# Width-one attention: queries and keys in one product over 128 partitions, and a shorter overflow test in the FP8 rounding

## What is computed

```
qkv = jnp.einsum('bnc,fc->bnf', x, w_qkv)
q, k, v = jnp.split(qkv, 3, axis=-1)          # each [b, n, 64]; a head is one column
dots = jnp.einsum('bhid,bhjd->bhij', q, k) * scale
dots = jnp.where(causal, dots, -jnp.inf)
attn = jax.nn.softmax(dots, axis=-1)
out = jnp.einsum('bhij,bhjd->bhid', attn, v)
return jnp.einsum('bnh,ch->bnc', out, w_out)
```

## Time and profile before

| what | us |
|---|---|
| median of 3 runs | 3184.69 |
| fastest and slowest of them | 3184.56, 3190.02 |
| the profiled execution | 3187.42 |
| its span (first to last instruction) | 3185.5 |
| mean granted TensorE clock, share of 2.4 GHz | 0.964 |
| L2_attn, groups of batches 0 to 7 in the trace, about | 1753 to 2045 |

### The profile page before, as it was taken

How to read it: one execution, slowest core, us unless ns; L and a number is a source line. 1 busy time by engine, 2 the same in 40 slices (tenths; PEclk the granted TensorE clock), 3 DMA queues, 4 the chain that set the end, 5 groups by cost and what they waited for, 6 DMA issues and landing times.

```text
span 3185.5 us, 52273 instructions
## 1 busy us (share of the span) xinstructions
PE 2957.7 (93%) x20671; PEld 1962.3 (62%) x20671; DVE 1873.6 (59%) x6456; ACT 1253.8 (39%) x1944; POOL 431.2 (14%) x458
## 2 busy tenths in 40 slices
PE   7999999988989889988998899998999999998998
PEld 4666666865555456655665556566667666766653
DVE  5534343699999447775678768574243444434455
ACT  2222222336555433323443668644233333323443
POOL 0010010124343310000000346410000000000000
PEclk9999999999999999999999779899999999998999
DMA  3000000010000100000000010100000000000000
GB/s 128 1 1 0 1 0 1 1 52 2 1 1 2 34 32 1 1 5 1 1 2 10 19 35 21 48 2 27 1 1 1 1 0 1 1 0 9 2 1 27
DMA packets 22028, 37.75 MB, mean 12 GB/s; under 512 B 2132, under 2 KB 19733, under 8 KB 20760
## 3 DMA queue, kind: packets, MB, share of 16 engines
q1 hardware_dynamic: 20968, 34.02, 3.2%
q10 hardware_dynamic: 816, 0.39, 0.1%
HBM read 26.81 MB, written 2.10 MB: 9 GB/s over the span
## 4 chain that ended last, share of the span: by engine, by line
PE 77%; DVE 16%; ACT 4%; issue 2%; DMA 0%; SPq 0%; DVEq 0%; POOL 0%; ACTq 0%; POOLq 0%
PE ps L414 45%; DVE arena L567 4%; PE ps L619 2%; PE ps L3040 2%; PE ps L2356 2%; PE ps L515 2%; PE ps L3059 2%; PE ps L2310 2%; PE ps L685 2%; ACT arena L673 2%; PE ps L1590 2%; PE ps L726 2%; DVE arena L1924 2%; PE ps L2913 1%; PE ps L552 1%
## 5 line engine op out<-in xcount | busy, mean ns | idle before, releaser
L414 PE MATMUL ps<-weights,arena 128*128 128x256 f32 (+4 forms) x2480 | 694.9, 430 | 41.5 <-DVE arena L1805 26.1
L414 PEld LDWEIGHTS ps<-weights,arena 128*128 128x128 f32 (+1 forms) x2480 | 462.8, 196 | 205.4 <-issue 94.2
L414 PE MATMUL ps<-arena,weights 128*128 128x256 f32 (+4 forms) x1726 | 562.3, 474 | 14.8 <-DMA weights<-in_w_L_attn 6.1
L414 PEld LDWEIGHTS ps<-arena,weights 128*128 128x128 f32 (+1 forms) x1726 | 317.4, 192 | 219.1 <-issue 155.8
L414 PE MATMUL ps<-arena 128*128 128x256 f32 (+4 forms) x1618 | 426.6, 417 | 6.0 <-ACT arena L4758 1.5
L414 PEld LDWEIGHTS ps<-arena 128*128 128x128 f32 (+2 forms) x1618 | 298.1, 188 | 115.1 <-issue 74.7
L567 DVE TENSOR_REDUCE arena<-ps 128x16 f32<-128x1232 f32 (+2 forms) x96 | 179.1, 1865 | 145.3 <-PE ps L545 47.9
L673 ACT ACTIVATE arena<-ps 77x2048 f32<-77x2048 f32 (+1 forms) x112 | 210.0, 1875 | 120.4 <-PE ps L619 58.4
L1924 DVE MATCH_REPLACE8 arena<-arena 128x77 f32<-128x77 f32 x1024 | 214.4, 225 | 0.0
L2323 ACT ACTIVATE arena<-ps 128x1536 f32<-128x1536 f32 x128 | 185.6, 1451 | 70.4 <-PE ps L2312 63.9
L854 POOL TENSOR_TENSOR x<-x,weights 128x512 f32<-128x512 f32 x32 | 43.8, 1370 | 1201.1 <-DVE arena L820 1153.3
(11 more groups left out here) (429 smaller groups left out, 4452.1 us busy)
## 6 DMA issues: line engine op xcount, KB each, us to landing
arena<-arena SPq DMA_DIRECT2D x156, 32.0 KB
weights<-in_w_L_ffn SPq DMA_DIRECT2D x1, 3848.0 KB, 11.6
weights<-in_w_L_attn SPq DMA_DIRECT2D x1, 3840.0 KB, 15.0
weights<-in_w_L_xattn SPq DMA_DIRECT2D x3, 1024.0 KB, 6.3
weights<-in_w_L_ffn SPq DMA_DIRECT2D x1, 3072.0 KB, 9.9
x<-in_x SPq DMA_DIRECT2D x2, 1024.0 KB
weights<-in_w_L_xattn SPq DMA_DIRECT2D x1, 2048.0 KB, 7.4
out<-x SPq DMA_DIRECT2D x8, 256.0 KB, 2.2
```

Source lines behind the costliest of these rows:

```text
L414: ins = k.nc.tensor.matmul(out, lhsT, rhs, start=start and i == 0, stop=i == n - 1)
```

## The change

1. Queries and keys become one product: 128 columns of `wqkv` as weights, queries on partitions 0 to 63, keys on 64 to 127, 256 columns. The copy is 128 x 256 instead of 64 x 512, the scans read partitions 64 to 127 and write 0 to 63.
2. The bounds are folded: tokens 0 to 127 on partitions 0 to 63, tokens 128 to 255 on partitions 64 to 127, by two instructions of 64 x 128. The block to split is 128 x 384 instead of 64 x 768.
3. The bounds' rows take two DMAs for each part instead of one (24 for a batch, 15 of them in ACT's list for batch 0), with pieces of 256 B instead of 512 B.
4. In batches 2 to 5 the bound parts stand at groups 9, 13, 13, 14, 15 instead of 9, 10, 13, 13, 14.
5. `kmax` and `kmin` get places of their own; a gap keeps every later buffer where it was.
6. The rounding's last part is two instructions instead of four: multiply by 2^128/464 (which overflows just where rounding does) and by 0, and add. `f_step` and `f_prep` count two fewer.

```
+OVERFLOW = 2.0 ** 128 / 464
 def round_last_vector(k, link, power, near, out):
     v = k.nc.vector
-    link(v.tensor_tensor(power, near, near, ALU.mult))
-    link(v.tensor_scalar(power, power, 448.0 ** 2, BIG, ALU.is_gt, ALU.mult))
-    link(v.tensor_scalar(power, power, BIG, 0.0, ALU.mult, ALU.mult))
+    link(v.tensor_scalar(power, near, OVERFLOW, 0.0, ALU.mult, ALU.mult))
     return v.tensor_tensor(out, power, near, ALU.add)
...
-ROWS_DMAS = 2 * PAIRS + PARTS
+ROWS_DMAS = 2 * PAIRS + 2 * PARTS
...
-            parts=c.take(PARTS, 3, SEQ, dt=BF16), qkm=c.take(3, SEQ), rest=c.take(3, SEQ)
+            parts=c.take(PARTS, SEQ + P, dt=BF16), qkm=c.take(SEQ + P), rest=c.take(SEQ + P),
+            kmax=c.take(SEQ), kmin=c.take(SEQ), gap=c.take(832)
...
 def rows_of_part(k, s, eng, n, i, queues):
+    q, key = s.parts[0:NH1, i, 0:SEQ], s.parts[NH1:P, i, 0:SEQ]
     for j in range(PARTS):
         if "k" in queues:
-            eng.dma_start(krows[PARTS * i + j:P:PAD, :, :], part[:, 1, :]).then_inc(rows, 16)
+            eng.dma_start(krows[PARTS * i + j:P:PAD, :, :], key).then_inc(rows, 16)
         if "q" in queues:
-            eng.dma_start(qrows[PARTS * j + i:P:PAD, :, :], part[:, 0, :]).then_inc(rows, 16)
+            eng.dma_start(qrows[PARTS * j + i:P:PAD, :, :], q).then_inc(rows, 16)
     if "q" in queues:
-        eng.dma_start(qrows[PAIRS + i:P:PAD, :, :], part[:, 2, :]).then_inc(rows, 16)
+        for half in (0, 1):
+            eng.dma_start(qrows[PAIRS + i:P:PAD, :, half * P:(half + 1) * P],
+                          s.parts[half * NH1:(half + 1) * NH1, i, SEQ:SEQ + P]).then_inc(rows, 16)
...
 def step_qk_tensor(k, pe, s, n, b):
     pe.wait_ge(*s.sig.at("zT", 0, n, 1))
-    for i in (0, 1):
-        ins = proj_feature(k, k.ps[0:NH1, b, i * SEQ:(i + 1) * SEQ], w_of(k, s.stage, "wqkv", KC), s.zT[n % 2],
-                           i * NH1, NH1)
-    ins.then_inc(*s.sig.up("qk_ps"))
+    proj_feature(k, k.ps[:, b, 0:SEQ], w_of(k, s.stage, "wqkv", KC), s.zT[n % 2], 0, 2 * NH1).then_inc(*s.sig.up("qk_ps"))
...
-    v.tensor_copy(s.qkm[0:NH1, 0:2, :], cut(k.ps[0:NH1, b, :], c=2)).then_inc(*s.sig.up("qk"))
+    v.tensor_copy(s.qkm[:, 0:SEQ], k.ps[:, b, 0:SEQ]).then_inc(*s.sig.up("qk"))
...
-        v.tensor_tensor(out, kmax, kmin, ALU.min).then_inc(*done)
+        for half in (0, 1):
+            at = slice(half * P, (half + 1) * P)
+            ins = v.tensor_tensor(s.qkm[half * NH1:(half + 1) * NH1, SEQ:SEQ + P], kmax[:, at], kmin[:, at], ALU.min)
+        ins.then_inc(*done)
...
-    x, rest, parts = s.qkm[0:NH1], s.rest[0:NH1], s.parts[0:NH1]
+    x, rest, parts = s.qkm, s.rest, s.parts
...
-BOUND_AT = (9, 10, 13, 13, 14)
+BOUND_AT = (9, 13, 13, 14, 15)
```

More of the change, by code:

```diff
@@ L1036, in fp8_signals @@
 def fp8_signals():
-    return dict(f_norm=13, f_z=1, f_zT_ps=1, f_zT=1, f_step=9, f_q=1, f_out_ps=1, f_scaled=1, f_shifted=1)
+    return dict(f_norm=13, f_z=1, f_zT_ps=1, f_zT=1, f_step=7, f_q=1, f_out_ps=1, f_scaled=1, f_shifted=1)
 def fp8_buffers(c):
@@ L1134, in turned_two_plan @@
                     done=1, stats=1, **narrow_signals(a), **narrow_signals(b), **fp8_signals())
-    s.ready = Signals(k.signals, st, 1, 1, f_prep=27, f_kernel=1)
+    s.ready = Signals(k.signals, st, 1, 1, f_prep=25, f_kernel=1)
     k.stats_ready["L1_ffn"] = s.sig.at("stats", 0, B - 1, 1)
@@ L2241, in width_one_plan @@
     two = (0, 1)
-    s = Bag(stage=st, z=c.take(2, D), zT=[c.take(KC, SEQ) for _ in two], parts=c.take(PARTS, 3, SEQ, dt=BF16),
-            qkm=c.take(3, SEQ), rest=c.take(3, SEQ), v=[c.take(2, NH1) for _ in two], seen=c.take(P),
+    s = Bag(stage=st, z=c.take(2, D), zT=[c.take(KC, SEQ) for _ in two], parts=c.take(PARTS, SEQ + P, dt=BF16),
+            qkm=c.take(SEQ + P), rest=c.take(SEQ + P), kmax=c.take(SEQ), kmin=c.take(SEQ), gap=c.take(832),
+            v=[c.take(2, NH1) for _ in two], seen=c.take(P),
             krows=[c.take(16, SEQ, dt=BF16) for _ in two],
@@ L2249, in width_one_plan @@
     assert low.at <= HALF, low.at
-    s.kmax, s.kmin = s.rest[:, 0, :], s.rest[:, 1, :]
     s.sig = Signals(k.signals, st, B, 1, z=1, zT_ps=1, zT=1, qk_ps=1, qk=1, v_ps=1, v=1, put=2, parts=PARTS, s_ps=GROUPS,
@@ L2272, in rows_of_part @@
     rows = s.moved.sems["rows"][0]
-    part, qrows, krows = s.parts[0:NH1, i], s.qrows[n % 2], s.krows[n % 2]
+    qrows, krows = s.qrows[n % 2], s.krows[n % 2]
+    q, key = s.parts[0:NH1, i, 0:SEQ], s.parts[NH1:P, i, 0:SEQ]
     eng.wait_ge(*s.sig.at("parts", 0, n, i + 1))
@@ L2486, in step_qk_scalar @@
     act.wait_ge(*s.sig.at("qk_ps", 0, n, 1))
-    k.nc.scalar.activation(s.qkm[0:NH1, 0:2, :], cut(k.ps[0:NH1, b, :], c=2), ACT.Copy).then_inc(*s.sig.up("qk"))
+    k.nc.scalar.activation(s.qkm[:, 0:SEQ], k.ps[:, b, 0:SEQ], ACT.Copy).then_inc(*s.sig.up("qk"))
 def step_v_scalar(k, act, s, n, b):
@@ L2541, in step_qk_vector @@
         dve.wait_ge(*s.sig.at("parts", 0, n - 1, PARTS))
-    v.tensor_copy(s.qkm[0:NH1, 0:2, :], cut(k.ps[0:NH1, b, :], c=2)).then_inc(*s.sig.up("qk"))
+    v.tensor_copy(s.qkm[:, 0:SEQ], k.ps[:, b, 0:SEQ]).then_inc(*s.sig.up("qk"))
 def step_bound_vector(k, dve, s, n, i):
     v, done = k.nc.vector, s.sig.up("split")
-    q, key, out = (s.qkm[0:NH1, j, :] for j in range(3))
+    q, key = s.qkm[0:NH1, 0:SEQ], s.qkm[NH1:P, 0:SEQ]
     kmax, kmin = s.kmax[0:NH1], s.kmin[0:NH1]
```

## The result

| what | us |
|---|---|
| kernel before, median of 6 runs (lowest, highest) | 3185.57 (3184.44, 3190.02) |
| changed kernel, median of 6 runs (lowest, highest) | 3206.55 (3204.84, 3214.23) |
| ratio, 95% interval | 1.0069 (1.0056 to 1.0081) |
| the profiled execution of the changed kernel, its span | 3209.55, 3207.7 |

The change makes the kernel 21 us, or 0.7%, slower. The forecast was 3162 and the range ended at 3189: wrong in sign, and outside.

A forecast was written before the change was run, and what follows sets the result against it. PE was taken to bound, DVE only in short stretches before the clock falls. Terms 0.25 - 0.6 - 1.84 - 1.4 - 16.7 - 0.94 - 2.8 + 1.2 = -22.8 took 3187.42 to 3164.6, median 2.7 below: 3162 us, range 3154 to 3189.

The forecast's parts named there:

- halved product of queries and keys: TensorE step of each batch, eight records become four: saves 0.94 us at full clock, 1.54 for batch 4 at low clock.
- rival C: Slower, clock doesn't come back behind the shortened products: one miss 3183 us, chance 0.08; two or more, 3208, chance 0.10.
- term of -16.7: Batch 1's means to batch 4's product: no clock fall, so 37.8 us at low level become 21.1 at full.
- C's +6.3: First miss, batch 1 group 8: the 11.4 us from 1827.4 to 1838.8, with 2.9 of waits, run low.
- Product at full clock: Products of batches 5, 6 and 7, with PE full: each saves 0.94 us, 2.8 together.
- Batch 3's product and DVE up to the means: Batch 3's halved step saves 1.84 us; shorter copy and rounding save 1.4 of PE's 2.34 us wait at the means.
- ACT's extra DMAs: Start of L2_attn, batch 0: three more row DMAs push ACT's first exponentials by 1.75 us; first wait ends 0.25 later.
- DVE around 1803: Copy, bounds and rounding before PE's waits of 1.75 and 0.39 us: together -0.6 us, bounds 0 and -1.3.
- Copy and bounds: DVE: copy of queries and keys falls from 0.68 to 0.41 us; the bounds' last part, now two instructions, adds 0.1.
- Split: DVE, five instructions from 768 to 384 columns: -2.2 us of DVE for a batch, 0 on the path.
- From batch 1's to batch 2's product: Start of L2_attn: ACT's DMA push takes the 1.8 us PE and DVE save; first wait ends 0.25 us later.
- sum with the clock as before: Rival A, the clock falls as before: terms sum to -7.9 us, 3177 us (3173 to 3180), chance 0.30.

The follow-up runs named there:

- E1: Changed kernel with the product of queries and keys done twice in every batch: 3188.5 us, ratio 1.0007.
- E2: Changed kernel with the product of queries and keys done twice for batch 4 alone: 3183.49 us, ratio 0.9996.
- E3: Kernel before with the shorter rounding alone, the product keeping its two halves: 3173.96 us, ratio 0.9963.
- E6: Kernel before with the shorter rounding and the second scan of batch 1's bounds at group 13: 3165.89, 3168.06 and 3170.92 us, ratio 0.9939.
- E4: Changed kernel with the old rounding, so the attention part alone: 3209.4 us, ratio 1.0057.
- E5: Changed kernel with the second scan of batch 1's bounds moved from group 11 to 13: 3210.89 us, ratio 1.0074.
- E8: E6 with batch 6's rounding cut into smaller pieces spread over three groups: 3177.46 us, ratio 0.9972.

## Why the prediction was wrong

**What failed.** Two steps of the working, both about the clock. The larger: the halved product of queries and keys was counted by its own length alone (-0.94 or -1.54), as if the clock came back behind it as it had behind the whole one. Behind batch 4's it did not, and the row up to batch 5's product came out at +21.9 instead of -0.94. The working had this as rival C and gave it too small a chance.

The other is the term of -16.7 for a fall that would not come ("with 1.4 us less of waiting this one is no longer such a stretch, so I expect no fall"). Where -15.5 was foreseen, -0.6 came. The wait did shrink, 2.34 to 1.19 us, and PE was busy 2.11 of 3.30 us instead of 1.47; the clock fell behind it. One pair of examples had been read as if it set a boundary. E1 and E2 have the same wait (1.19) with a fall, E3 shows one of 1.17 without; E6 has one of 0.67 without and E3 one of 0.68 with one. None of these numbers predicts a fall. Had this term held, there would have been no low stretch for batch 4's step to end, and neither loss.

**The rival that came true.** C had the mechanism and nearly the price: a second miss was costed at "17.3 x 16/11 = 25 more", and it was 21.9 + 1.54 (what the step was to save there at the low level), 23.4; E2 says 23.1 by the medians, and 21.0 by its row from batch 4's to batch 5's product. It had the place a batch early: its first miss was to be batch 3's and its second batch 4's; in the profiled execution batch 3's step brought the clock back and batch 4's did not. In E4 and E5 both missed, as C had it, and there the first miss can be priced: from batch 3's to batch 4's product 51.5 us in both, 46.1 in the changed kernel, so 5.4. C's +6.3 does not follow from the numbers beside it (8.5 us of work at 17.3 in 20.5 give 7.2). Its total of 3208 is 1.5 us from the median, partly by luck: it has a miss of batch 3 (6.3 us) that the trace does not show, and does not have the 5.5 us that this execution already had at batch 1's product.

**What misled on its chance.** C got 0.10 for two misses. The argument against it was that the clock rose 1.5 us into a step of 2.73, so 1.84 us should do. A time inside a step at which the clock rises is no proof that the step up to there was the reason. The counter-evidence was cited too: nothing rose behind the 1.97 us step of values, and the halved step came out at 2.08. By the table above it brings the clock back about one time in two, so that, seen afterwards, with two low stretches that end on such a step a miss was the likelier outcome. The rule of the Trainium skill ("TensorE: Matmul & The Clock Gate", Part 1), that the throttled state is the default and activity releases it, pointed to the right side. The traces go together with its first half as far as the low stretches begin behind waits of PE (here 1.19 us). With its second they do not, as it stands: PE was busy 51.00 of 51.00 us from 1880, and nothing was released.

**The terms that held.**
- *Product at full clock*, -0.94: 30.30 to 29.49 between batches 6 and 7, -0.8. That four matmuls with 128 columns cost what four with 64 did holds: behind the first of a step each takes 377 to 380 ns at full clock and 634 at the low one, as before; the first takes 483 (430 before) and 796 (689). So the steps are 2.08 where 1.84 was foreseen and 1.13 where 0.94 was.
- *Batch 3's product and DVE up to the means*, -3.24: measured -3.2. Within it the wait ended at 1.19, not 0.9, and PE came to it sooner.
- *ACT's extra DMAs*: first exponentials 15.19 us behind batch 1's product instead of 13.61, +1.6 for 1.75 foreseen; taken up as worked out: PE, early by the shorter step, waited 3.78 us for the row DMAs (1.48 before). Up to the L727 at 1767.68 it is 19.77 us, 19.64 before: +0.1 for +0.25. The pieces of 256 B had no price that these traces show: from the end of ACT's last row DMA issue to the first scores it is 1.73 us, 2.75 before.
- *DVE around 1803*, -0.6: -0.5. The forms differ: one wait of 2.93 in place of 1.75 and 0.39.
- *Copy and bounds*: 0.42 for 0.41. Two minima take 0.83 us together on average (6.6 in eight batches) in place of 0.67, +0.16 for +0.1; in batch 2 it is 0.59 in place of 0.73.

**Sized wrong, off the path.** *Split*: the first cast takes 627 ns in place of 821, all five instructions together 3.5 us in place of 4.8: -1.3 for a batch, not -2.2.

**A small miss.** From batch 1's to batch 2's product +0.25 was foreseen and +1.0 came. Beside the start's +0.1, the step of tokens out at 1781.08 took 3.60 us instead of the 2.73 at 1775.41, since here the clock came back 3.3 us into the step, at 1784.4. It is again a term of the clock that the sum did not have.

**What the halves are worth.** Rounding alone: -11.3 us (E3). Attention alone: +24.1 by the median, about 0 at its lower level (E4). Both: +21.0. Both, with one step lengthened again: -1.8 (E2). The sum with the clock as before, 3177, is 6.5 below E2. Of this, 1.5 is batch 4's step, which E2 has in its old length; what makes up the other 5 is open. Nor do the halves simply add up: each changes what the other finds of the clock, and single executions of one kernel spread over 12 us and more (E1, E2, E3).

**Left open.** Why the same step, of the same length, brings the clock back in some executions and not in others; why the wait of 0.67 or 0.68 us is followed by a fall in one kernel and not in the other; what the other executions of the changed kernel lost, of which only one was profiled; and the 5.3 us by which that one was already late before the first changed instruction, in stages where the code is the same.

## What to carry to other kernels

Before a dense TensorE step (matmuls over all 128 rows, back to back) is made shorter, look at the granted clock around it: if the clock comes back behind that step, the step is worth what lies after it at low clock (here 22 us), not its own length (1.6). Cost both outcomes, and treat a single place where the clock held or rose as one example and no boundary. A part that looks small and lies on another engine (two DVE instructions, 1.11 us together) can be worth ten times its length if it shortens a low stretch, and parts of a change that both touch the clock are best timed one by one: here the good half (-11 us) hid behind the bad one.

## What was not expected of the hardware

- PE stayed at 1.2 GHz through 126 us of unbroken work (busy 125.97 of 126.00; E4, E5). The work was score matmuls over 32 rows, value matmuls with 32 columns of weights, and the short steps between.
- The same kernel settles at one of two levels some 25 us apart on one chip (E4: 3184 or 3210; E8: 3165 to 3171 or 3193 to 3196, and one run between). The median of a few runs of such a kernel can fall on either.
- Matmuls that compute nothing new made the changed kernel 23 us faster (E2), on a full PE.
